# Down product of the routed experts: two of its three blocks as three fp32r passes, index columns on VectorE, all expert weights through one load queue

## The reference

```python
def _mlp(x, gw, uw, dw):
    return jax.nn.silu(x @ gw.T) * (x @ uw.T) @ dw.T
rw = _route(x, gate_w, gate_bias)          # 8 of 64 experts per row, weights
expert_out = jax.vmap(lambda gw_, uw_, dw_: _mlp(x, gw_, uw_, dw_))(Wg, Wu, Wd)
routed = jnp.einsum('eth,te->th', expert_out, rw)
shared = _mlp(x, Sg, Su, Sd)
```

## Time and profile before

| | us |
|---|---|
| median of three runs | 1690.39 |
| lowest, highest | 1687.99, 1692.44 |
| the profiled execution, its own time | 1692.39 |
| its span, first to last instruction | 1690.4 |
| mean granted clock of TensorE | 0.992 |

### The profile page before, as it was taken

One profiled execution on the slowest core, in us unless ns is written; L12 is line 12 of the kernel. 1 busy time (PEld: TensorE's weight loads), 2 busy tenths in 40 slices (PEclk: granted clock), 3 DMA queues, 4 the chain that ended last, 5 costly groups with the idle time before them and its releaser, 6 DMA issues.

```text
span 1690.4 us, 35168 instructions
## 1 busy us (share of the span) xinstructions
PE 1637.6 (97%) x13779; PEld 1354.7 (80%) x13781; DVE 965.6 (57%) x2065; ACT 636.5 (38%) x845; POOL 446.5 (26%) x453
## 2 busy tenths in 40 slices
PE   8999999999999999899999999999999999999896
PEld 5666677777787777778998998989889899897583
DVE  3877577666666675554445454444444444444476
ACT  1232156666655665124324233242333422423021
POOL 3110255555555555111203013030030300300100
PEclk9999999999999999999999999999999999999898
DMA  8003399999999997202002011020010200202100
GB/s 301 13 6 114 134 368 334 344 329 331 343 342 343 340 323 243 91 1 67 19 2 79 7 47 38 1 80 6 25 56 6 79 7 2 79 1 101 57 1 26
DMA packets 68476, 214.91 MB, mean 127 GB/s; under 512 B 13107, under 2 KB 30771, under 8 KB 58497
## 3 DMA queue, kind: packets, MB, share of 16 engines
q1 hardware_dynamic: 38656, 153.03, 25.2%
q10 hardware_dynamic: 15360, 43.26, 7.4%
q0 software_dynamic: 14336, 16.83, 4.8%
HBM read 208.07 MB, written 21.76 MB: 136 GB/s over the span
## 4 chain that ended last, share of the span: by engine, by line
PE 93%; DVE 3%; ACT 2%; issue 1%; DMA 1%; POOL 0%; POOLq 0%; DVEq 0%; SPq 0%; ACTq 0%
PE PS L1299 18%; PE PS L1290 17%; PE PS L2077 14%; PE PS L2100 9%; PE PS L1317 6%; PE PS L1337 6%; PE PS L1354 3%; PE PS L385 3%; PE PS L741 2%; PE PS L443 2%; PE PS L2061 2%; PE PS L406 1%; PE PS L757 1%; PE PS L2089 1%; PE PS L1375 1%
## 5 line engine op out<-in xcount | busy, mean ns | idle before, releaser
L1299 PE MATMUL PS<-S_r 128*128 128x256 f32 x2496 | 327.8, 286 | 1.9 <-DVE kh0l L1492 1.9
L1299 PEld LDWEIGHTS PS<-S_r 128*128 128x128 f32 x2496 | 303.4, 189 | 28.9 <-issue 24.5
L1290 PE MATMUL PS<-S_r 128*128 128x384 f32 (+1 forms) x1536 | 308.0, 350 | 0.0
L2077 PE MATMUL PS<-S_r,R_r 128*128 128x352 f32 x1152 | 298.1, 349 | 1.7 <-DVE R_r L2216 1.7
L1290 PEld LDWEIGHTS PS<-S_r 128*128 128x128 f32 x1536 | 266.7, 188 | 10.7 <-DVE kh1l L1492 2.0
L2077 PEld LDWEIGHTS PS<-S_r,R_r 128*128 128x128 f32 x1152 | 198.9, 188 | 20.8 <-issue 18.5
L1450 ACT COPY S<-PS 128x512 f32<-128x512 f32 (+1 forms) x128 | 64.3, 502 | 269.5 <-PE PS L1337 269.5
L1230 POOL COPY S<-qbd 128x128 f32<-128x128 f32 x32 | 9.4, 293 | 584.6 <-PE PS L1317 572.0
L1503 DVE CUSTOM_DVE_ANT_0 R<-PS,maskadd 128x384 f32<-128x384 f32 (+1 forms) x256 | 136.1, 569 | 24.1 <-PE PS L1317 23.0
L1485 DVE TENSOR_TENSOR R<-PS,vbias 128x256 f32<-128x256 f32 (+1 forms) x208 | 87.9, 423 | 96.0 <-PE PS L1299 91.7
L1213 POOL TENSOR_TENSOR S_r<-S,S_r 128x1536 fp32r<-128x1536 f32 (+2 forms) x31 | 113.7, 3687 | 77.5 <-ACT S_r L1421 77.4
(11 more groups left out here) (261 smaller groups left out, 2469.2 us busy)
## 6 DMA issues: line engine op xcount, KB each, us to landing
R<-in_w_gu SPq DMA_DIRECT2D x34, 1408.0 KB, 17.3
R<-in_w_dna ACTq DMA_DIRECT2D x45, 512.0 KB
qbd<-in_w_gu SPq DMA_DIRECT2D x16, 1408.0 KB
S<-in_w_gu SPq DMA_DIRECT2D x16, 1408.0 KB
S<-in_ctxT SPq DMA_DIRECT2D x24, 768.0 KB, 4.6
R<-in_w_dnb ACTq DMA_DIRECT2D x45, 192.0 KB
xnT<-in_w_dna ACTq DMA_DIRECT2D x15, 512.0 KB
S<-in_ctxT SPq DMA_DIRECT2D x8, 898.0 KB, 6.3
```

Of the source, the lines that this page charges most:

```text
L1290: last = nc.tensor.matmul(PS[:, bank, 0:n], w3[0][:, cc, f0:f0 + P], x3[i][:, cc, 0:n], start=(cc == 0 and w3 is wkv_hi and x3 is ctx_hi), ...
L1299: last = nc.tensor.matmul(PS[:, bank, 0:256], x3[need][:, cc, k0:k0 + P], w3[1][:, cc, f0:f0 + 256], start=(cc == 0 and w3 is wkv_hi and x ...
L2077: last = nc.tensor.matmul(PS[:, gu, 0:I], x3[:, c, :], w3[:, c, gu, :], start=(c == 0 and x3 is hi[0] and w3 is hi[1]), stop=(c == NC - 1 ...
```

## The change

The 128-row blocks of the down product become three fp32r passes each (six matmuls of 512 columns), and the 96-row block stays fp32 and runs first. ACT rounds the two blocks of a tile's down weights (`down_high`, 128 x 1024, into a buffer per parity of the tile) and of the turned hidden tile (`hidden_high`, which also copies the 96-row block), and DVE makes the rests (`down_low` in place, `hidden_low`). The down weights are loaded by SP for all tiles, behind the gate/up weights of the next tile and after a wait for the down product of four tiles before. POOL's two column copies per tile go; DVE writes both columns for tile k in one copy (`columns`), one iteration ahead for the gather. Two subtractions on POOL (`rest`, weights of the next stage) move ahead of the first gathers. In the last tile, ACT's `hidden_high` stands behind two roundings of context chunks.

```diff
...
-        gcol = sb("gcol", [P, NBUF], I32)
-        scol = sb("scol", [P, NBUF], I32)
+        cols = sb("cols", [P, NBUF, 2], I32)
...
+        m = Arena(kq[:, :])
+        wdn_hi = [m.view(2, D) for _ in range(2)]
+        hT_lo = m.view(2, P)
...
+            dve.wait_ge(tables, 1)
+            nc.vector.tensor_copy(cols[:, :, 1], idx_tab[:, 0:NBUF]).then_inc(cols_set, NBUF)
...
+                def load_dn(r, k):
+
+                    i = NBUF * r + k
+                    ev = expert(r, k)
+                    if not (isinstance(r, int) and r == 0):
+                        sp.wait_ge(y_made, i - NBUF + 1)
...
-                with sp.Fori(1, n) as r:
+                for k in range(NBUF):
+                    load_gu(1, k)
+                    if k:
+                        load_dn(1, k - 1)
+                with sp.Fori(2, n) as r:
                     for k in range(NBUF):
-                        load(r, k)
+                        load_gu(r, k)
+                        load_dn(*tile_before(r, k))
+                load_dn(n - 1, NBUF - 1)
...
                 def gather(r, k):
...
-                    nc.gpsimd.tensor_copy(gcol[:, k:k + 1], idx_tab[:, column(r, k)]).then_inc(gcol_set, 1)
-                    col_set = count(pool, i + 1)
-                    pool.wait_ge(tables, 1)
-                    pool.wait_ge(gcol_set, col_set)
+                    pool.wait_ge(cols_set, col_set)
...
                 def scatter(r, k):
...
-                    nc.gpsimd.tensor_copy(scol[:, k:k + 1], idx_tab[:, column(r, k)]).then_inc(scol_set, 1)
-                    col_set = count(pool, i + 1)
-                    pool.wait_ge(tables, 1)
-                    pool.wait_ge(scol_set, col_set)
+                    pool.wait_ge(cols_set, col_set)
...
                 first_pool(pool)
+                for i in range(2):
+                    rest(wkv_lo[i], slot[1 + 2 * i], wkv_hi[i], w_lo, w_hi, i + 1)
                 n = iterations(pool)
                 for k in range(NBUF):
                     gather(0, k)
-                for i in range(2):
-                    rest(wkv_lo[i], slot[1 + 2 * i], wkv_hi[i], w_lo, w_hi, i + 1)
...
-                    for j, (i0, w) in enumerate(IJ):
-                        last = nc.tensor.matmul(PS[:, 3, :], hT[0:w, j, :], wdn[k][0:w, j, :],
-                                                start=(j == 0), stop=(j == 2))
+                    nc.tensor.matmul(PS[:, 3, :], hT[0:IJ[2][1], 2, :], wdn[k][0:IJ[2][1], 2, :], start=True, stop=False)
+                    pe.wait_ge(dl_ready, i + 1)
+                    for j in range(2):
+                        for h3, w3 in ((hT_hi, wdn_hi[k % 2]), (hT_lo, wdn_hi[k % 2]), (hT_hi, wdn_lo[k])):
+                            last = nc.tensor.matmul(PS[:, 3, :], h3[:, j, :], w3[:, j, :],
+                                                    start=False, stop=(j == 1 and w3 is wdn_lo[k]))
...
-                def load_down(r, k):
...
+                def hidden_high(r, k):
+
+                    i = NBUF * r + k
+                    act.wait_ge(ht_made, i + 1)
+                    if not (isinstance(i, int) and i == 0):
+                        act.wait_ge(y_made, i)
+                    nc.scalar.copy(hT[0:96, 2, :], PS[0:96, 2, 2 * P:3 * P])
+                    nc.scalar.copy(hT_hi, PS[:, 2, 0:2 * P].rearrange("p (a b) -> p a b", a=2)).then_inc(hh_ready, 1)
+
+                def down_high(r, k):
+
+                    i = NBUF * r + k
+                    act.wait_ge(w_dn[k], 32 * (r + 1))
+                    if not (isinstance(r, int) and r == 0 and k < 2):
+                        act.wait_ge(y_made, i - 1)
+                    nc.scalar.copy(wdn_hi[k % 2], wdn[k][:, 0:2, :]).then_inc(dh_ready, 1)
...
                 def step(r, k, final=False):
                     silu(r, k)
+                    if not (isinstance(r, int) and r == 0 and k == 0):
+                        hidden_high(*tile_before(r, k))
                     if not (final and k == NBUF - 1):
                         rows_high(*tile_after(r, k))
+                    down_high(r, k)
                     if not (final and k >= NBUF - 2):
                         weights_high(*tile_after(*tile_after(r, k)))
                     if not (isinstance(r, int) and r == 0 and k == 0):
                         rows_out_copy(*tile_before(r, k))
-                        if not (final and k):
-                            load_down(*(tile_before(r + 1, k) if k else (r, NBUF - 1)))
...
                 silu(n - 1, NBUF - 1)
+                hidden_high(n - 1, NBUF - 2)
+                down_high(n - 1, NBUF - 1)
                 act.wait_ge(u_made, NBUF * n - 1)
                 ctx_high(0, 0)
                 act.wait_ge(u_made, NBUF * n)
                 ctx_high(0, 1)
+                hidden_high(n - 1, NBUF - 1)
...
-                def hidden_copy(r, k):
+                def hidden_low(r, k):
                     i = NBUF * r + k
-                    dve.wait_ge(ht_made, i + 1)
+                    dve.wait_ge(hh_ready, i + 1)
...
-                    nc.vector.tensor_copy(hT[:, 0:2, :], PS[:, 2, 0:2 * P].rearrange("p (a b) -> p a b", a=2))
-                    nc.vector.tensor_copy(hT[0:96, 2, :], PS[0:96, 2, 2 * P:3 * P]).then_inc(ht_ready, 1)
+                    nc.vector.tensor_tensor(hT_lo, PS[:, 2, 0:2 * P].rearrange("p (a b) -> p a b", a=2),
+                                            hT_hi.bitcast(F32), ALU.subtract).then_inc(ht_ready, 1)
+
+                def down_low(r, k):
+
+                    dve.wait_ge(dh_ready, NBUF * r + k + 1)
+                    nc.vector.tensor_tensor(wdn_lo[k], wdn[k][:, 0:2, :], wdn_hi[k % 2].bitcast(F32),
+                                            ALU.subtract).then_inc(dl_ready, 1)
+
+                def columns(r, k, final):
+
+                    dve.wait_ge(xg_loaded[k], 16 * r)
+                    if not (isinstance(r, int) and r < 2):
+                        dve.wait_ge(y_added[k % 2], 16 * (scatters_before(r - 2, k) + 1))
...
+                        last = nc.vector.tensor_copy(cols[:, k, :], pairs[:, k, at])
+                    last.then_inc(cols_set, 1)
...
                     if not (isinstance(r, int) and r == 0 and k == 0):
-                        hidden_copy(*tile_before(r, k))
+                        hidden_low(*tile_before(r, k))
                     if not (final and k == NBUF - 1):
                         rows_low(*tile_after(r, k))
+                    columns(r + 1, k, final)
                     mul(r, k)
+                    down_low(r, k)
...
```

More of the change, by code:

```diff
@@ L66, in perceiver @@
         x = sb("x", [P, NT, D])
-        xnT = sb("xnT", [P, NC, T])
+        with nc.sbuf_tensor("xnT", [P, NC, T], F32) as xnT:
+            pass
+        xnT_r = sb("xnT_r", [P, NC, T], F32R)
         with nc.sbuf_tensor("qbd", [P, NC, B, P], F32) as qbd:
@@ L140, in perceiver @@
         idle = Arena(flat(xnT[:, :, :]))
+        dn_at = m.at
         wdn = [m.view(3, D), idle.view(3, D)] + [m.view(3, D) for _ in range(2)]
+        wdn_lo = [Arena(R0_r, dn_at).view(2, D), Arena(flat(xnT_r[:, :, :])).view(2, D)]
+        wdn_lo += [Arena(R0_r, dn_at + i * 3 * D).view(2, D) for i in (1, 2)]
         m.view(NC, P)
@@ L222, in perceiver @@
         qraw, qzero = (R1[:, 2 * NC * SP + i * P:2 * NC * SP + (i + 1) * P] for i in range(2))
-        kh = [[sb(f"kh{i}{half}", [P, KN[3]], F32R) for half in "hl"] for i in range(2)]
-        qb = [[sb(f"qb{i}{half}", [P, P], F32R) for half in "hl"] for i in range(2)]
+        kq = sb("kq", [P, 4 * KN[3] + 4 * P], F32R)
+        kh = [[kq[:, (2 * i + half) * KN[3]:(2 * i + half + 1) * KN[3]] for half in range(2)] for i in range(2)]
+        qb = [[kq[:, 4 * KN[3] + (2 * i + half) * P:4 * KN[3] + (2 * i + half + 1) * P] for half in range(2)]
+              for i in range(2)]
+        m = Arena(kq[:, :])
+        wdn_hi = [m.view(2, D) for _ in range(2)]
+        hT_lo = m.view(2, P)
         wkv_hi, wkv_lo = ([square(S_r, slot_at(i), NC) for i in ii] for ii in ((0, 2), (1, 3)))
@@ L1946, in _, with expert, load_gu @@
             def _(sp):
-                def load(r, k):
+                def expert(r, k):
+                    return bass.ds(sp.value_load(eot_row[0:1, column(r, k)], min_val=0, max_val=E - 1), 1)
+                def load_gu(r, k):
                     i = NBUF * r + k
-                    e = sp.value_load(eot_row[0:1, column(r, k)], min_val=0, max_val=E - 1)
-                    ev = bass.ds(e, 1)
-                    if not isinstance(r, int):
+                    ev = expert(r, k)
+                    if not (isinstance(r, int) and r == 0):
                         sp.wait_ge(u_made, i - NBUF + 1)
@@ L1957, in load @@
                                  a["w_gu2"][ev, :, :].rearrange("e p n -> (e p) n")).then_inc(w_gu[k], 16)
-                    if not isinstance(r, int):
-                        return
-                    if k == 1:
+                def load_dn(r, k):
```

(38 more changed lines are left out.)

16 lines of the change are left out of this document (8 added, 8 removed).

## The result

| | median | lowest to highest | ratio to before |
|---|---|---|---|
| before | 1692.07 us (8 runs) | 1687.04 to 1695.1 | |
| changed | 1685.93 us (8 runs) | 1679.04 to 1688.86 | 0.9962, 95% interval 0.9947 to 0.9977 |

The change makes the kernel 0.4% faster. I had predicted 1666 us, with a range from 1660 to 1683: the result is 20 us above the forecast and outside the range. The profiled execution took 1682.99 us, its span 1681.2.

What follows compares the result with a forecast made beforehand. It took TensorE (PE) to bound the expert stage, 64 tiles of 7.20 us. PE saving -25.6, last tile +0.3, loads +1 us: 1668.1 from the profiled 1692.39, 1666 against the median; range 1660 to 1683.

Steps and rivals of the forecast that it cites:

- the part on the DMA side: Expert-stage weight loads: at 384 GB/s on one queue a tile needs 6.80 us, nearly but not quite the bound; 1 us charged.
- The store: Gate/up loads issued two tiles ahead: up to 7.6 us of lateness can build up over the expert stage before PE waits.
- 60 x 0.14 us: Expert-stage loads at 375 GB/s: shortest tile 6.94 us, so 8.4 us more than PE needs, of which 7.6 is absorbed.
- The fp32r product: Down product on PE: six fp32r matmuls at 0.22 us replace 1.72 us of fp32, saving 0.40 us a tile, 25.6 us.
- DVE and ACT fit: Expert tile: the added work of ACT and DVE fits in 6.80 us, with 0.75 and 0.3 us of room, at no cost.
- the second rival: Expert tile: DVE or ACT binds, tile 6.93 us (1673 us) or 7.37 us (10 us slower than before); chance 0.10.
- The tail: Last expert tile: ACT rounds context chunks before copying the last hidden tile; +0.3 us, bounds 0 and 2.
- Loads bound the stage: First rival, expert stage: at 366 GB/s the tile cannot go under 7.08 us, so 1676 to 1683 us; chance 0.24.
- The slower case, one queue serving worse than two: Third rival, expert-stage loads under 351 GB/s lengthen the stage; at 340, tile 7.53 us and 1702 us; chance 0.07.
- The fp32r product was faster: Answers the last rival, in the down product: fp32r no faster than two fp32 passes, +55 us; chance 0.01.

Runs made afterwards that it cites:

- e6: Changed kernel with only the third down block's load padded by zeros from 96 to 128 rows, still two down loads: 1670.22 us (0.9872).
- e4: Changed kernel with a tile's down weights in one load of 128 rows of 6144 bytes, third block zero-padded, instead of two loads: 1669.7 us (0.9868).
- e7: As e4, but a tile's gate/up weights come in two loads of 5632-byte rows instead of one of 11264-byte rows: 1669.07 us (0.9868).
- e8: As e4, but with the two matmuls of the low hidden rows left out of each down product: 1657.76 us (0.9802).
- e12: Changed kernel with its 96-row load, the two matmuls of the low hidden rows left out of each down product: 1685.19 us (0.996).

## Why the prediction was wrong

**The step that failed** is the last one of the part on the DMA side: "I expect the loads to be nearly but not quite the bound, and charge 1 us". The loads are the bound, and they cost 16 us: 1685.93 less the 1669.7 of the kernel that differs in its down loads alone. The rest of the sum holds: 1666 less that 1 us, plus the 4.5 us of the fp32r term below, is 1669.5, and the kernels with 128 rows took 1669.1 to 1670.7.

The working went wrong where it preferred one row to another. The earlier trace rows gave 366 GB/s for the loads in the stage itself, and so a shortest tile of 7.08 us; the run with less matmul work measured 7.14. I set against it the 400, 369 and 395 GB/s of three short windows and took 384 for "one queue". They differ from the stage in what was loaded. By SP's issues (start us, us) in the kernel before, no third block is in flight until 172.23 us:

```profile
171.18 0.35 SPq L1956 DMA_DIRECT2D qbd<-in_w_gu  x1
171.72 0.33 SPq L1964 DMA_DIRECT2D R<-in_w_dna  x1
172.23 0.33 SPq L1966 DMA_DIRECT2D R<-in_w_dnb  x1
```

Of the two windows behind it, the one from 174 to 177 us (400 GB/s) has no packet of 2048 bytes, and the one from 177 to 180 (369) has all 96 of the third block's. The third window, at 395, holds one 96-row load and, beside it, the 1 MB copy of x into the accumulator (L1975, issued at 213.27), so it was not loads alone. That reading is made afterwards; what the runs show is that with 128 rows one queue does give 381 to 393 GB/s of its own time, and with 96 rows 353 to 357, or 369 when the tile is 7.20 us and the engines are a little less pressed (one-queue kernel before: 127.40 MB in 81.4%). An average rate of the stage with its own mix of loads was the better estimate than the best of a few windows.

**The store.** Right in kind: lateness built up unseen. ACT's first wait for a load ends at 327.45 us, after some 16 tiles:

```profile
327.45 2.64 ACT L1943 CAST S_r<-R 128x1408 fp32r<-128x1408 f32 x2 [1.95 <-DMA R<-in_w_gu]
```

At 7.14 to 7.20 us a tile for the loads, 16 x 0.26 to 0.32 = 4 to 5 us had been absorbed by then, not 7.6. The 60 x 0.14 us behind it should have been worked out at 7.08, not at the 6.94 of a rate that no row of the stage had.

**The fp32r product**, 0.222 us from the rows of 352 and 450 columns, bounds 0.20 and 0.24, was mis-sized a little. Its weight loads (start us, us):

```profile
285.26 0.19 PEld L2124 LDWEIGHTS PS<-kq 128*128 128x128 f32 x1 [0.24 <-issue]
285.50 0.19 PEld L2124 LDWEIGHTS PS<-xnT_r,R_r 128*128 128x128 f32 x1
285.73 0.19 PEld L2124 LDWEIGHTS PS<-kq,R_r 128*128 128x128 f32 x1
285.96 0.19 PEld L2124 LDWEIGHTS PS<-kq 128*128 128x128 f32 x1
286.19 0.19 PEld L2124 LDWEIGHTS PS<-xnT_r,R_r 128*128 128x128 f32 x1
286.42 0.19 PEld L2098 LDWEIGHTS PS<-S_r,R_r 128*128 128x128 f32 x1
```

0.232 us each, six are 1.39 us, saved 0.33 a tile instead of 0.40: 64 x 0.07 = 4.5 us. PE's tile is 6.88, not 6.80. The slope between 352 and 450 columns, 0.41 ns a column, was carried on to 512; from 450 to 512 it was (0.232 - 0.196) / 62 = 0.58 ns.

**DVE and ACT fit**, as laid out. One tile of the changed kernel (start us, us, engine, line):

```profile
287.14 0.68 ACT L2182 ACTIVATE x<-PS,w_tab 128x512 f32<-128x512 f32 x1
288.78 0.47 ACT L2171 ACTIVATE R<-PS 128x352 f32<-128x352 f32 x1 [0.97 <-PE PS L2098]
289.14 0.25 ACT L2190 COPY R<-PS 96x128 f32<-96x128 f32 x1
289.29 0.38 ACT L2191 CAST R_r<-PS 128x256 fp32r<-128x256 f32 x1
289.70 0.42 DVE L2260 TENSOR_TENSOR kq<-PS,R_r 128x256 fp32r<-128x256 f32 x1 [0.32 <-ACT R_r L2191]
290.03 1.07 ACT L2199 CAST kq<-R 128x1024 fp32r<-128x1024 f32 x1
290.19 0.69 DVE L2251 TENSOR_TENSOR R_r<-PS,R_r 128x512 fp32r<-128x512 f32 x1
290.80 0.16 DVE L2279 COPY cols<-idx_tab 128x2 int32 x1
```

Hidden rows 0.25 and 0.38 (taken as 0.26 and 0.37), rounding of the down weights 1.07 (1.03), hidden low 0.42 (0.42), columns 0.16 (0.15). ACT waits 0.97 us for PE ahead of its silu, so there was room. With the loads mended PE has no gap, so neither engine binds: the second rival is out.

**The tail** was charged 0.3 us: PE waits 1.30 us ahead of the last down product instead of 0.71, 0.6 more, within its bounds. The stage behind it came out 2.1 us shorter: 959.31 us from its 32 matmuls at 707.95 to the last ones at 1667.26 before, 957.24 from 700.76 to 1658.00 after. The granted clock goes with it. The two executions have the same spells at the lower level (0.50, that is 1.2 GHz) but for one: it lasts 6.8 us in the kernel before and 3.4 in the changed one, after 10.6 us in which PE was busy 7.17 and 6.57 us. From inside that spell (columns as the earlier trace rows):

```profile
1563.60:1570.30 6.70, 5.74 (x11) 2.93 (x11) 1.15 (x3) 1.41 (x3) 0.00 (x0) 0.50 0.00 0
```

```profile
1557.30:1560.60 3.30, 3.03 (x7) 1.93 (x8) 1.15 (x3) 0.69 (x3) 0.00 (x0) 0.50 0.00 0
```

Of the two versions with a padded third block, the one with 6.8 us (e6) took 959.34 for this stretch and the one with 3.4 (e4) 957.15. So the 2.1 us are no effect of the change on that stage.

**The rivals.** "Loads bound the stage" had the mechanism, with 7.08 us for 7.14 and with 1676 to 1683 us for 1686; its shortest tile was 0.06 us too low, 60 x 0.06 = 3.6 us. The slower case, one queue serving worse than two, is not what happened at 7.20 us a tile (ratio 0.9996), but once the loads bind, down loads on a second queue, issued at another moment, are worth 6 us (1679.8 against 1685.9); why is open. The fp32r product was faster, as the rows said. The page "DMA: Bandwidth & Descriptors" of the Trainium skill gave 7.12 us a tile by its 358 GB/s. The changed kernel's mean tile is 7.12, but by another cause: the kernels with one down load moved 357 GB/s over 424 us without a wait for a load (e4, e7), and 384 over 200 us with less matmul work (e8), so the traces disagree with 358 GB/s as a limit.

## What to carry to other kernels

When a change shortens a stage whose DMA share is already 0.99, the shortest tile that the loads allow, at the rate of the stage itself, is the first number to work out, and the forecast should be the larger of it and the compute tile. A load that fills only part of the partitions is suspect there: here, padding 96 rows to 128 cost 3% more bytes and made the kernel 16 us faster. To find what a stage's loads allow, cut the compute work and look where the tile stops.

## What the runs showed of the hardware that was not expected

- The DMA share does not show how much more could be moved. From 226 to 650 us it was 1.01 in the changed kernel at 337 GB/s and 1.00 in the kernel with one down load at 357. The same gate/up rows stay longer in the engines when a 96-row load is beside them: the mean packet of 11264 bytes took 493 ns in the changed kernel and 465 in the one that differs by the padding alone (e6).
- 64 rows on partitions 0 to 63 disturb the other loads more than 64 rows on 0 to 31 and 64 to 95 (1676.5 against 1658.4 us; 498 against 484 ns for the mean packet of 11264 bytes). The second place is not free: with the full 128-row load (e8) it is 463 ns. The Trainium skill ("SBUF — State Buffer", Door 1: The DMA port swizzle) says that partitions 0 to 63 reach no more DMA ports than 0 to 31 do, eight of sixteen, and that 64 to 127 reach the other eight. The three kernels with 64 rows agree with it.
- By that rule a 96-row load puts 64 rows on one half of the ports and 32 on the other; padding adds rows to the emptier half only, so the fuller half has as much to do as before, and yet all loads get faster (357 to 385 GB/s; mean packets of 2048, 4096 and 11264 bytes from 103, 179 and 493 ns to 85, 168 and 465). The fuller half alone does not explain that. How the rows are dealt out to the engines may do so; no run here shows it, and it stays open.
- The rate in the middle of the stage is lower than at its start in the kernels that the loads bound: 384 GB/s from 226 to 426 us and 353 from 526 to 600 in e8, 348 from 226 to 326 and 335 from 526 to 600 in e12. This, too, is open.
